# A Mamba-2 layer on one core: in the steps without an early convolution tile, the late tile is multiplied before the state's product

## The chip, the cores and the metric

One core of a Trainium2 chip. The time is the device time of one launch in microseconds (us), the median of three runs. TensorE is called PE in the profile (PEld is its weight load), VectorE is DVE, ScalarE is ACT, GpSimd is POOL and SyncE, which issues the transfers, is SP.

## The reference

The layer takes x of 2 batches by 1024 tokens by 512 channels, all float32, and returns x + s * g. Cut to what matters:

```python
xn = layernorm(x)
proj = xn @ in_proj_w.T                      # gate 4096, hbc 6144, dt 64
xBC = silu(conv_bias + sum_k pad(hbc)[k:k+L] * conv_weight[:, k])   # 4 taps over time
x, Bm, Cm = split(xBC)                       # 64 heads x 64, 8 groups x 128, 8 groups x 128
dt = softplus(dt + dt_bias); dA = exp(dt * -exp(A_log))
# over time, for each head:
state = state * dA_t + (dt_t * x_t) outer B_t
y_t = state @ C_t
y = y + x * D
yn = rms_norm_by_group(y) * norm_weight * silu(gate)
s = yn @ out_proj_w.T
g = silu(xn @ W.T + bias + lora(xn))
out = x + s * g
```

## The kernel before, in words

After a first stage (the first 125 us or so: layer norm, the gate g, the step sizes) the kernel runs a main loop of 128 steps i. A step is one chunk of 128 tokens of one group of 8 heads; 8 steps are the 1024 tokens of one group in one batch. In this document the groups are counted 0 to 15 in the order in which they run, and the place of a step in its group is 0 to 7: step i is group i // 8, place i % 8. Group 7 and group 8 differ from the others: in group 7 and the first steps of group 8 the finished rows of the first batch are also multiplied, added and stored by POOL (`fin_multiply`, `fin_add`), and the normalised input of the other batch is fetched.

Each engine runs its own instructions in the order in which they are written, and waits on semaphores for the others. The orders are written out by hand. In step i PE does, in this order:

- the output projection of chunk i-2 into `ps_out` (12 matmuls, waits for `ynt_hi` and `ynt_lo` of that chunk)
- `ps_y`, the outputs of chunk i-1 from the decay matrix and from the state before it (L1219, L1224; waits for `decay` by DVE L906 and for `cpre` by POOL L1027)
- the sum of squares of chunk i-2 (L1231), the transpose of B for chunk i (L1238)
- the early convolution tile, if the step has one (12 matmuls into `ps_conv`)
- a gate tile (12 matmuls into `ps_gate`)
- the state's product into `ps_s` (L1250, two matmul records of 128x512)
- the late convolution tile, if the step has one (12 matmuls into `ps_conv`)
- the transposes of x for chunk i+1 into `turned_x` (L1174), and C times B into `ps_g` (L1260)

Twelve matmuls are three passes of four (L1074, L1077, L1080 with L1081 for the last one), which is how a float32 product is made of split operands. The convolution's projection of the next block of 512 tokens has six tiles, spread over the four steps of the block before it: `conv_early(i)` gives one tile where i % 4 is 1, 2 or 3, `conv_late(i)` gives one where i % 4 is 0, 1 or 2. So steps at places 0 and 4 have a late tile and no early one, places 3 and 7 an early one and no late one, and places 1, 2, 5 and 6 have both. The last block of all has no next block, so steps 124 to 127 have no convolution tile.

The state's product of step i waits for `b_tok` (ACT), for `xw` (DVE L861) and for `S["state"]` of step i-1: the same bank `ps_s` holds the product of the step before until DVE has added it to the state (L872; L875 where the group begins). There is no `ps_s` product at place 7. DVE does in step i: the taps of the late tile of step i-1 (L753), `dtx` (L848), a scan of `decay` (L852), `last` (L857), `xw`, then for step i-1 `ps_y` plus `skip` (L866, waits for POOL's `skip`, L1056), `state` (L872), the product with the gate (L883), `out_sum` (L894), `ynt_lo` (L898), then the taps of the early tile and `decay` times `ps_g` (L906, waits for PE's L1260). POOL does in step i: `rstd_col` (L1009), the low halves of the weights where the place is 1, 3, 4, 5 or 6 (`wconv_lo` L918 of the next group at places 3 and 5, `wgate_lo` L924 at 4 and 6), `cpre`, two sums of squares (L1033, L1036), the decayed state (L1048) and `skip`. The convolution tile at place 4 is the first that needs the next group's `wconv_lo`.

Of the kernel before, what the change touches and what calls it, by code (L numbers as in the profile page):

```python
# [31 lines left out]
N = NB * CPB  # L32
# [55 lines left out]
def conv_early(i):  # L88

    nb, r = i // CPB + 1, i % CPB  # L90
    return nb * MT + 2 * r - 1 if r and nb < NB else None


def conv_late(i):
    nb, r = i // CPB + 1, i % CPB
    return nb * MT + 2 * r if r < CPB - 1 and nb < NB else None


def taps_done(k):

    return (TAPS - 1) * (k + 1)


def tile_of(k):
    nb, at = divmod(k, MT)
    m = tile_order(nb)[at]
    g, blk = nb // NBLK % GROUPS, nb % NBLK
    return nb, m, blk, g * MT + m
# [16 lines left out]
def build(nc, hidden, w_in_t, conv_w, conv_b, dt_bias, a_log, d_skip, norm_w, w_out_t,  # L125
          lora_a, lora_b_t, w_ffn_t, ffn_bias, lora_w, out):
    ctx = ExitStack()
    with ctx:
# [937 lines left out]
        def _(e):  # L1066
            w = Waits(e)

            def passes(ps, a, b, n, second, third, done):


                (a_hi, a_lo), (b_hi_, b_lo_) = a, b
                for t in range(n):
                    e.matmul(ps, a_hi(t), b_hi_(t), start=t == 0, stop=False)  # L1074
                second()
                for t in range(n):
                    e.matmul(ps, a_lo(t), b_hi_(t), start=False, stop=False)  # L1077
                third()
                for t in range(n - 1):
                    e.matmul(ps, a_hi(t), b_lo_(t), start=False, stop=False)  # L1080
                e.matmul(ps, a_hi(n - 1), b_lo_(n - 1), start=False, stop=True).then_inc(done, 1)  # L1081
# [17 lines left out]
            def conv(k):  # L1099
                nb, m, blk, tile = tile_of(k)  # L1100
                g = nb // NBLK
                ready = NCH + (blk + 1) * CPB
                if m < XT:
                    w.wait_ge(S["hi_cx"], KT * (g + 1))
                else:
                    w.wait_ge(S["hi_cbc"], KT * (g + 1))
                w.wait_ge(S["hi"], ready)
                if nb >= NB // 2:
                    w.wait_ge(landed_xn[blk], 32 * CPB)

                def w_lo_ready():
                    w.wait_ge(S["lo_cx"] if m < XT else S["lo_cbc"], KT * (g + 1))

                def xn_lo_ready():
                    w.wait_ge(S["lo"], ready)

                w.wait_ge(S["taps"], taps_done(k - 2))
                passes(ps_conv[k % 2][:, :], weights(wconv_hi, wconv_lo, chunk_cols(m)),
                       xn_cols(slice(blk * BLK, (blk + 1) * BLK)), KT, w_lo_ready, xn_lo_ready, S["mm_conv"])

            def rate(q, part):
                b, j = RATES[q]
                if part == 0:
                    ready = (0 if b == 1 else NCH) + (j + 1) * CPB
                    w.wait_ge(S["hi_dt"], KT)
                    w.wait_ge(S["hi"], ready)
                    w.wait_ge(S["z"], q)
                    passes(ps_out[:, :], weights(wout_hi, wout_lo, slice(0, P)),
                           xn_cols(slice(j * BLK, (j + 1) * BLK)), KT,
                           lambda: w.wait_ge(S["lo_dt"], KT), lambda: w.wait_ge(S["lo"], ready), S["mm_dt"])  # L1130
                elif part == 5:
                    ds = rate_rooms(q)[3]
                    w.wait_ge(S["pfx"], q + 1)
                    w.wait_ge(S["pt"], q)
                    if q == 3:
                        w.wait_ge(S["state"], 3)
                    for i in range(CPB - 1):
                        e.transpose(ps_s[:, i * P:(i + 1) * P], ds[:, i * P:(i + 1) * P], eye)
                    e.transpose(ps_s[:, (CPB - 1) * P:], ds[:, (CPB - 1) * P:], eye).then_inc(S["mm_pt"], 1)
# [52 lines left out]
            for i in range(N + DRAIN):  # L1192
                m, u = i - 1, i - DRAIN
                xb, cc = xc[i // CPB % 2], block_cols(i % NCH)
                cm, gm = m % NCH, group(m)
                if u >= 0:
                    gu = group(u)
                    w.wait_ge(S["z"], len(RATES))
                    w.wait_ge(S["osum"], u)
                    w.wait_ge(S["hi2"], u + 1)  # L1200
                    w.wait_ge(S["hi_out"], XT * (gu + 1))
                    passes(ps_out[:, :], (lambda t: ynt_hi[:, t, :], lambda t: ynt_lo[:, t, :]),
                           weights(wout_hi, wout_lo, slice(0, DM)), XT,
                           lambda: w.wait_ge(S["lo2"], u + 1), lambda: w.wait_ge(S["lo_out"], XT * (gu + 1)),
                           S["mm_out"])
                if 0 <= m < N:
                    mx, dx = decay[m % 3], dtx[m % 2]
                    w.wait_ge(S["M"], m + 1)
                    w.wait_ge(S["biased"], TOK)
                    w.wait_ge(S["dtx"], m + 1)  # L1210
                    w.wait_ge(S["lo2"], m)
                    if cm > 0:
                        w.wait_ge(S["state"], inner(m - 1))
                        w.wait_ge(S["cpre"], later(m))
                        before, c_left = state[(gm + cm - 1) % 2], cpre[(later(m) - 1) % 2]
                    for two in range(0, GH, 2):
                        for h in (two, two + 1):
                            y_h = ps_y[h % 2 * HD:(h % 2 + 1) * HD, h // 2 * P:(h // 2 + 1) * P]
                            mixed = e.matmul(y_h, dx[:, h * HD:(h + 1) * HD], mx[:, h * P:(h + 1) * P], start=True,  # L1219
                                             stop=cm == 0, skip_group_check=True)  # L1220
                        if cm > 0:
                            for h in (two, two + 1):
                                y_h = ps_y[h % 2 * HD:(h % 2 + 1) * HD, h // 2 * P:(h // 2 + 1) * P]
                                mixed = e.matmul(y_h, before[:, h * HD:(h + 1) * HD], c_left[:, h, :], start=False,  # L1224
                                                 stop=True, skip_group_check=True)
                    mixed.then_inc(S["mm_in"], 1)
                if u >= 0:
                    w.wait_ge(S["eye"], 3)
                    w.wait_ge(S["sum2"], u + 1)
                    w.wait_ge(S["M"], min(i, N))  # L1230
                    e.matmul(ps_g[:, 2 * P:2 * P + 1], square_sum[:, :], ones[:, :], start=True, stop=True,  # L1231
                             skip_group_check=True).then_inc(S["mm_ssq"], 1)
                if i < N and i % NCH < NCH - 1:
                    w.wait_ge(S["silu"], conv_no(i // CPB, XT) + 1)
                    w.wait_ge(S["M"], i)
                    w.wait_ge(S["var2"], u if u >= 0 else 0)
                    w.wait_ge(S["lo"], TOK)
                    e.transpose(ps_g[:, 0:P], xb[:, XT, cc], eye).then_inc(S["mm_bt"], 1)  # L1238
                if i < N and conv_early(i) is not None:
                    conv(conv_early(i))  # L1240
                for k in gated(i):
                    gate(k)
                if i == 3:
                    rate(3, 5)
                if i < N and i % NCH < NCH - 1:
                    w.wait_ge(S["pt"], 3 if i < 3 else 4)
                    w.wait_ge(S["b_tok"], inner(i))
                    w.wait_ge(S["xw"], inner(i))
                    w.wait_ge(S["state"], inner(m) if m >= 0 else 0)
                    e.matmul(ps_s[:, :], b_tok[:, :], xw[:, :], start=True, stop=True).then_inc(S["mm_u"], 1)  # L1250
                if i < N and conv_late(i) is not None:
                    conv(conv_late(i))
                if i + 1 < N:
                    turn_xc(i + 1)
                if i < N:
                    w.wait_ge(S["silu"], conv_no(i // CPB, XT + 1) + 1)
                    w.wait_ge(S["var2"], u + 1 if u >= 0 else 0)
                    if i % NCH < NCH - 1:
                        w.wait_ge(S["b_tok"], inner(i))
                    e.matmul(ps_g[:, P:2 * P], xb[:, XT, cc], xb[:, XT + 1, cc], start=True, stop=True,  # L1260
                             skip_group_check=True).then_inc(S["mm_g"], 1)
# [39 lines left out]
```

## Time and profile before

| | |
|---|---|
| median of 3 runs | 1868.99 us (1868.94 to 1869.1) |
| the profiled execution's own time | 1868.11 us |
| its span, first to last instruction | 1866.3 us |
| mean granted TensorE clock | 0.990 |
| PE busy | 96% of the span |
| PEld busy | 76% |
| DVE busy | 82% |
| POOL busy | 62% |
| ACT busy | 45% |
| PE's share of the chain that ended last | 77%, POOL 12% |

Busy time counts an instruction from its start to its end; the ends of matmuls are modelled and overlap the next one, so the distance from one start to the next is the better measure of what a matmul costs. "Idle before" in brackets is the time an engine stood still before an instruction, and the arrow names who released it.

### The profile page before, as it was taken

To read this page: it belongs to the slowest core of one execution; us is meant where nothing else is said; L and a number is where in the kernel's file an instruction comes from. 1 tells how busy PE (TensorE), PEld (TensorE's weight loads), DVE (VectorE), ACT (ScalarE), POOL (GpSimd) and SP (SyncE) were. 2 spreads that over 40 slices of the span, in tenths; PEclk is the share of its full clock that TensorE was granted. 3 is DMA by queue.
4 is the path that set the end of the run, shared out by engine and by line. 5 is a ranking of instruction groups with operands and counts; after the bars stand their busy time and mean duration, and the time that the engine had idled before them with its cause. 6 is when DMAs were issued, how large, how long until landed. Compare 5 with 4: busy or idle time off the path is not lost.

```text
span 1866.3 us, 29427 instructions
## 1 busy us (share of the span) xinstructions
PE 1799.7 (96%) x10904; PEld 1426.0 (76%) x10904; DVE 1524.5 (82%) x1960; ACT 835.2 (45%) x1806; POOL 1152.4 (62%) x1137
## 2 busy tenths in 40 slices
PE   6888999999999999999999999999999999999995
PEld 4766787878777777877777787777878788787874
DVE  6748788888888888888888878888888888888885
ACT  4865444443535444353534444354444435444431
POOL 4125757475575657566597756647574765857478
PEclk9998999999999999999999999999999999999998
DMA  7432423323232333323465333323233323323333
GB/s 246 151 103 70 148 77 130 102 102 106 98 136 102 102 102 102 124 95 132 148 203 181 119 113 108 119 91 115 89 116 111 124 103 102 135 77 106 102 114 124
DMA packets 113502, 220.70 MB, mean 118 GB/s; under 512 B 10448, under 2 KB 46672, under 8 KB 113360
## 3 DMA queue, kind: packets, MB, share of 16 engines
q1 hardware_dynamic: 112320, 218.66, 35.0%
q8 instruction: 87, 1.43, 0.3%
q14 instruction: 55, 0.45, 0.1%
q10 hardware_dynamic: 1040, 0.16, 0.0%
HBM read 204.63 MB, written 14.16 MB: 117 GB/s over the span
## 4 chain that ended last, share of the span: by engine, by line
PE 77%; POOL 12%; DVE 4%; issue 3%; ACT 2%; DMA 1%; SPq 0%; POOLq 0%; DVEq 0%; ACTq 0%
PE ps_conv L1074 9%; PE ps_conv L1077 8%; PE ps_conv L1080 6%; PE ps_y L1219 6%; PE ps_out L1074 5%; PE ps_out L1077 5%; PE ps_gate L1074 5%; PE ps_gate L1077 5%; PE ps_s L1250 4%; PE ps_y L1224 4%; PE ps_out L1080 4%; PE ps_gate L1080 4%; POOL wconv_lo L918 3%; PE turned_x L1174 2%; POOL state L1048 2%
## 5 line engine op out<-in xcount | busy, mean ns | idle before, releaser
L1009 POOL TENSOR_TENSOR rstd_col<-mean_square,half 128x1 f32<-128x1 f32 x128 | 107.2, 837 | 567.2 <-ACT mean_square L666 567.2
L753 DVE SCALAR_TENSOR_TENSOR xc<-ps_conv,convw_sb,xc 128x511 f32<-128x511 f32 (+2 forms) x576 | 429.6, 746 | 24.8 <-ACT xc L552 10.7
L906 DVE TENSOR_TENSOR decay<-decay,ps_g 128x1024 f32<-128x1024 f32 x128 | 156.0, 1218 | 199.0 <-PE ps_g L1260 199.0
L852 DVE TENSOR_TENSOR_SCAN decay<-decay,eye 128x1024 f32<-128x1024 f32 x128 | 297.8, 2327 | 0.8 <-DMA decay<-decays_d 0.8
L558 ACT ACTIVATE xc<-xc 128x512 f32<-128x512 f32 x192 | 121.3, 632 | 375.0 <-DVE xc L753 374.2
L1027 POOL TENSOR_TENSOR cpre<-cpre,xc 128x1024 f32<-128x1024 f32 x112 | 268.0, 2393 | 0.0
L1074 PE MATMUL ps_conv<-xn_hi,wconv_hi 128*128 128x512 f32 x768 | 256.3, 456 | 0.0
L1077 PE MATMUL ps_conv<-xn_hi,wconv_lo 128*128 128x512 f32 x768 | 207.2, 392 | 0.0
L1219 PE MATMUL ps_y<-decay,dtx 128*64 128x128 f32 x2048 | 197.3, 279 | 1.7 <-DVE decay L906 1.7
L1074 PEld LDWEIGHTS ps_conv<-xn_hi,wconv_hi 128*128 128x128 f32 x768 | 140.9, 193 | 62.9 <-issue 45.3
L675 ACT ACTIVATE square<-ps_y 128x512 f32<-128x512 f32 x128 | 76.7, 600 | 240.6 <-DVE ps_y L866 240.6
L1224 PE MATMUL ps_y<-cpre,state 128*64 128x128 f32 x1792 | 174.1, 273 | 0.0
L1077 PEld LDWEIGHTS ps_conv<-xn_hi,wconv_lo 128*128 128x128 f32 x768 | 144.9, 189 | 32.7
L1080 PE MATMUL ps_conv<-xn_lo,wconv_hi 128*128 128x512 f32 x576 | 162.3, 390 | 0.0
L1219 PEld LDWEIGHTS ps_y<-decay,dtx 128*64 128x64 f32 x2048 | 120.9, 136 | 48.4 <-issue 46.0
L1074 PE MATMUL ps_out<-wout_hi,ynt_hi 128*128 128x512 f32 x512 | 151.6, 418 | 4.6 <-DVE out_sum L894 4.6
L552 ACT ACTIVATE xc<-ps_conv,convb_sb,convw_sb 128x512 f32<-128x512 f32 (+1 forms) x192 | 150.2, 782 | 0.0
L1074 PE MATMUL ps_gate<-xn_hi,wgate_hi 128*128 128x512 f32 x512 | 141.4, 398 | 4.8 <-ACT wgate_hi L510 2.8
L918 POOL TENSOR_TENSOR wconv_lo<-stage,wconv_hi 128x512 fp32r<-128x512 f32 (+1 forms) x128 | 126.2, 1013 | 27.6 <-ACT wconv_hi L502 27.6
L1250 PE MATMUL ps_s<-xw,b_tok 128*128 128x512 f32 x224 | 118.9, 612 | 24.7 <-DVE state L872 16.8
L1077 PE MATMUL ps_out<-wout_hi,ynt_lo 128*128 128x512 f32 x512 | 140.8, 397 | 0.0
L1077 PE MATMUL ps_gate<-xn_hi,wgate_lo 128*128 128x512 f32 x512 | 138.0, 392 | 0.0
(192 smaller groups left out, 3743.8 us busy)
## 6 DMA issues: line engine op xcount, KB each, us to landing
decay<-decays_d SPq DMA_DIRECT2D x128, 512.0 KB, 5.2
cpre<-rows_d SPq DMA_DIRECT2D x112, 512.0 KB, 3.9
stage<-w_in_t SPq DMA_DIRECT2D x32, 1024.0 KB, 6.4
stage<-w_out_t SPq DMA_DIRECT2D x16, 1024.0 KB, 5.3
stage<-w_in_t SPq DMA_DIRECT2D x32, 256.0 KB, 3.4
out_sum<-hidden SPq DMA_DIRECT2D x16, 256.0 KB, 5.5
ffn_d<-sgate SPq DMA_DIRECT2D x16, 256.0 KB, 2.0
io<-ffn_d SPq DMA_DIRECT2D x16, 256.0 KB, 3.8
```

Of the source, the lines that this page charges most:

```text
L552: e.activation(acc[:, first:], ps[:, first:], ACT.Identity, bias=convb_sb[:, tile, 0:1], scale=tap).then_inc(S["tap0"], 1)
L753: e.scalar_tensor_tensor(acc[:, d:], ps[:, 0:BLK - d], convw_sb[:, tile, TAPS - 1 - d:TAPS - d], acc[:, d:], ALU.mult, ALU.add).then_inc(S ...
L852: e.tensor_tensor_scan(d[:, :], d[:, :], eye8[:, :, :].rearrange("p h i -> p (h i)"), 0.0, ALU.mult, ALU.add).then_inc(S["scan"], 1)
L906: e.tensor_tensor(by_head(d[:, :]), by_head(d[:, :]), ps_g[:, P:2 * P].unsqueeze(1).to_broadcast([P, GH, P]), ALU.mult).then_inc(S["M"], 1)
L918: e.tensor_tensor(lo[:, t, :], raw[:, t, :], hi[:, t, :].bitcast(F32), ALU.subtract).then_inc(done, 1)
L1027: e.tensor_tensor(cpre[k % 2][:, :, :], cpre[k % 2][:, :, :], xc[i // CPB % 2][:, XT + 1, block_cols(i % NCH)].unsqueeze(1).to_broadcast([ ...
L1074: e.matmul(ps, a_hi(t), b_hi_(t), start=t == 0, stop=False)
L1077: e.matmul(ps, a_lo(t), b_hi_(t), start=False, stop=False)
L1080: e.matmul(ps, a_hi(t), b_lo_(t), start=False, stop=False)
L1219: mixed = e.matmul(y_h, dx[:, h * HD:(h + 1) * HD], mx[:, h * P:(h + 1) * P], start=True, stop=cm == 0, skip_group_check=True)
L1224: mixed = e.matmul(y_h, before[:, h * HD:(h + 1) * HD], c_left[:, h, :], start=False, stop=True, skip_group_check=True)
L1250: e.matmul(ps_s[:, :], b_tok[:, :], xw[:, :], start=True, stop=True).then_inc(S["mm_u"], 1)
```

## The change

In a step that has a late convolution tile and no early one, the late tile's 12 matmuls are issued right after the gate tile, and the state's product behind them. In all other steps the order stays. Only PE's order changes; no instruction is added or removed, and each keeps its waits.

```diff
                 if i == 3:
                     rate(3, 5)
+                late_first = i < N and conv_early(i) is None and conv_late(i) is not None
+                if late_first:
+                    conv(conv_late(i))
                 if i < N and i % NCH < NCH - 1:
                     w.wait_ge(S["pt"], 3 if i < 3 else 4)
                     w.wait_ge(S["b_tok"], inner(i))
                     w.wait_ge(S["xw"], inner(i))
                     w.wait_ge(S["state"], inner(m) if m >= 0 else 0)
                     e.matmul(ps_s[:, :], b_tok[:, :], xw[:, :], start=True, stop=True).then_inc(S["mm_u"], 1)
-                if i < N and conv_late(i) is not None:
+                if i < N and conv_late(i) is not None and not late_first:
                     conv(conv_late(i))
```

## Rows read from the trace of the kernel before

**Rows 1.** The page's busy time of each engine, with its share of the span.

```profile
PE 1799.7 (96%) x10904; PEld 1426.0 (76%) x10904; DVE 1524.5 (82%) x1960; ACT 835.2 (45%) x1806; POOL 1152.4 (62%) x1137
```

**Rows 2.** Window over group 3: its length, then busy PE, PEld, DVE, ACT, POOL.

```profile
682.95:790.51 107.56, 106.97 (x662) 85.15 (x661) 90.06 (x114) 47.69 (x107) 67.37 (x68) 1.00 0.33 109
```

**Rows 3.** Who waited for whom, PE: total us, times, longest.

```profile
PE ps_s L1250 <- DVE state L872: 16.8, 18, 2.6
```

**Rows 4.** The chain that ended last, in order of time, group 2, places 3 and 4.

```profile
617.88 2.52 POOL wconv_lo L918 x2
...
626.94 1.04 POOL skip L1056
```

**Rows 5.** Timeline of PE at group 2, place 4: start, duration, instruction, idle before.

```profile
628.54 0.39 PE L1081 MATMUL ps_gate<-xn_lo,wgate_hi 128*128 128x512 f32 x1
629.52 1.10 PE L1250 MATMUL ps_s<-xw,b_tok 128*128 128x512 f32 x2 [0.59 <-DVE state L872]
630.05 1.49 PE L1074 MATMUL ps_conv<-xn_hi,wconv_hi 128*128 128x512 f32 x4
...
633.22 0.60 PE L1174 MATMUL turned_x<-eye,xc 128*128 128x128 f32 x4
```

**Rows 6.** Timeline of PE at place 4 of group 0 and of group 8, same two ends.

```profile
197.82 0.39 PE L1081 MATMUL ps_gate<-xn_lo,wgate_hi 128*128 128x512 f32 x1
...
202.86 0.60 PE L1174 MATMUL turned_x<-eye,xc 128*128 128x128 f32 x4
...
1059.39 0.39 PE L1081 MATMUL ps_gate<-xn_lo,wgate_hi 128*128 128x512 f32 x1
...
1064.53 0.60 PE L1174 MATMUL turned_x<-eye,xc 128*128 128x128 f32 x4
```

**Rows 7.** Timeline of PE at group 3, place 0, same two ends.

```profile
682.71 0.40 PE L1081 MATMUL ps_gate<-xn_lo,wgate_hi 128*128 128x512 f32 x1
...
686.55 0.60 PE L1174 MATMUL turned_x<-eye,xc 128*128 128x128 f32 x4
```

**Rows 8.** Timeline of PE at group 2, place 7: a gate tile behind a convolution tile.

```profile
671.62 1.07 PE L1074 MATMUL ps_gate<-xn_hi,wgate_hi 128*128 128x512 f32 x4
...
674.34 0.60 PE L1174 MATMUL turned_x<-eye,xc 128*128 128x128 f32 x4
```

**Rows 9.** Timeline of PE at group 2, place 3: the transposes behind the state's product.

```profile
619.29 1.02 PE L1250 MATMUL ps_s<-xw,b_tok 128*128 128x512 f32 x2
...
620.15 0.60 PE L1174 MATMUL turned_x<-eye,xc 128*128 128x128 f32 x4
```

**Rows 10.** Timeline of DVE and POOL from group 2, place 4 on.

```profile
628.69 0.68 DVE L872 TENSOR_TENSOR state<-ps_s,state 128x512 f32<-128x512 f32 x1
...
630.81 0.69 DVE L898 TENSOR_TENSOR ynt_lo<-ps_y,ynt_hi 128x512 fp32r<-128x512 f32 x1
...
634.08 1.22 DVE L906 TENSOR_TENSOR decay<-decay,ps_g 128x1024 f32<-128x1024 f32 x1 [2.58 <-PE ps_g L1260]
...
635.51 1.04 POOL L1056 TENSOR_TENSOR skip<-xc,dskip_sb 128x512 f32<-128x512 f32 x1
...
638.03 2.28 DVE L852 TENSOR_TENSOR_SCAN decay<-decay,eye 128x1024 f32<-128x1024 f32 x1
...
640.55 0.69 DVE L861 TENSOR_TENSOR xw<-turned_x,last 128x512 f32<-128x512 f32 x1
```

**Rows 11.** Timeline of POOL, PE and DVE in group 7, places 4 and 6.

```profile
956.30 2.42 POOL L1027 TENSOR_TENSOR cpre<-cpre,xc 128x1024 f32<-128x1024 f32 x1
...
959.52 0.44 PE L1219 MATMUL ps_y<-decay,dtx 128*64 128x128 f32 x4
...
986.72 1.22 DVE L906 TENSOR_TENSOR decay<-decay,ps_g 128x1024 f32<-128x1024 f32 x1 [0.46 <-PE ps_g L1260]
```

**Rows 12.** Timeline at group 2, place 3: POOL's decayed state and DVE's scan.

```profile
623.70 2.44 DVE L852 TENSOR_TENSOR_SCAN decay<-decay,eye 128x1024 f32<-128x1024 f32 x1
...
623.96 3.02 POOL L1048 TENSOR_TENSOR state<-state,total_bc 128x512 f32<-128x512 f32 x1
```

## Prediction

> **What bounds the kernel now.** I read the page first: PE is busy 96% of the span, DVE 82%, POOL 62% [rows 1]. That makes PE the first candidate, but a share over the whole span hides where it stands still, so I went to windows of one group each. An ordinary group takes 107.56 us with PE busy for 106.97: 0.59 us of idle time in eight steps [rows 2]. So in the main loop the time is PE's instruction stream plus very few gaps, and the question is which gaps the change touches.
>
> The list of waits names the largest kind: the state's product waited for DVE's `state` (L872) 18 times, 16.8 us in all [rows 3]. I went through its timeline: 15 of the 18 stand at place 4, one in each of groups 0 to 14 (0.98 in group 0, 0.58 or 0.59 in thirteen groups, 1.05 in group 8). The three others are at step 2 (2.64) and at places 5 and 6 of the last group (2.49 and 2.00), and those steps keep their order. Place 4 stalls because it has only the gate tile ahead of the product, and because POOL is late there. The chain that ended last goes through POOL's `wconv_lo` until 620.40, then its other work up to `skip` until 627.98 [rows 4], DVE's `ps_y` and `state`, which ends at 628.69 + 0.68 = 629.37 [rows 10], and the product at 629.52 [rows 5].
>
> **The change, part by part.** Nothing is added or removed, so the sum consists of starts that move. I measure from the start of the gate tile's last matmul to the start of the transposes that close the sequence.
>
> Before, at an ordinary place 4: 628.54 to 633.22 = 4.68 us [rows 5]. The same instructions at place 0, where nothing waits: 682.71 to 686.55 = 3.84 [rows 7]. So the wait costs 4.68 - 3.84 = 0.84 in starts, more than its 0.59 of idle time, because idle time is counted only from the modelled end of the matmul before.
>
> After: a convolution tile straight behind a gate tile is in no row of this kernel. The nearest is the opposite, a gate tile behind a convolution tile at place 7, with the same shapes: 12 matmuls from 671.62 to 674.34, 2.72, or 0.227 each [rows 8]. From the gate tile's last start to the product are thus 13 such distances, 2.95. From the product to the transposes behind it, place 3 shows 619.29 to 620.15 = 0.86 [rows 9]. Together 3.81, if nothing waits. At place 0 that is 0.03 less than 3.84. The bound from below for the new handovers is no saving against 3.84. The other bound is that a convolution tile keeps the length that it has now behind the product: 630.05 to 633.22 is 3.17 [rows 5] instead of 2.72, so up to 0.45 a step more. I take 3.81, since rows 8 show two tiles of the same kind one behind the other.
>
> Now the wait. The product would start at 628.54 + 2.95 = 631.49, and `state` ends at 629.37: 2.1 us to spare, so all of the wait goes. Per place:
>
> - 13 ordinary groups: 4.68 - 3.81 = 0.87, times 13 = 11.3
> - group 0: 197.82 to 202.86 is 5.04 [rows 6]; minus 3.81 = 1.2
> - group 8: 1059.39 to 1064.53 is 5.14 [rows 6]; minus 3.81 = 1.3
> - place 0 in 16 groups: 16 x 0.03 = 0.5
> - sum: 14.3 us
>
> **What comes next where the stall was.** PE runs 0.87 ahead from place 4 on, and something could stop it there. The second pass of the output projection needs `ynt_lo`, finished at 630.81 + 0.69 = 631.50 [rows 10]; by then PE is only at the product. DVE's L906 stood idle 2.58 us waiting for PE [rows 10], so DVE moves ahead by the whole 0.87. POOL's `skip` for the next `ps_y` ends at 636.55 and DVE asks for it after `xw`, 641.24 before and 640.37 after [rows 10]. What waits for the product itself is DVE's `xw` of the next step (it may not be overwritten) and then `state`: the product ends at about 632.3, `xw` starts at 640.55 - 0.87 [rows 10], 7.3 us later. The tile that is moved ahead needs `wconv_lo`, ready at 620.40 [rows 4], against 628.77. No transfer is issued by PE and none waits for the product, so SP's queue keeps its order.
>
> Group 7 is tighter, because POOL also finishes the output rows there. At place 4 `cpre` ends at 958.72 and `ps_y` starts at 959.52; 0.87 earlier is 958.65 [rows 11], a new wait of 0.1. At place 6 DVE's L906 idles only 0.46 [rows 11], so DVE can follow PE by 0.46 and not by 0.87, and 0.4 is at stake at the next `ps_y`. I take 0.1 for group 7, and 0.5 as the other end.
>
> The row of the decayed state at place 3 shows POOL held up by DVE: it takes 3.02 us and overlaps the scan of 2.44 [rows 12], where `skip`, of the same size, takes 1.04 [rows 10]. Now DVE moves 0.87 against POOL, whose work around place 4 stays. The scan moves from 638.03 to 637.16 and `skip` ends at 636.55, so they stay apart by 0.6. The Trainium skill, page "SBUF — State Buffer", section "Who interferes with whom", says that a DVE instruction with two SBUF inputs and a GpSimd one that reads SBUF take turns, the later one blocked for the whole of the first. The trace agrees (3.02 against 1.04). By that rule the new overlap would be in group 7, where the sum would lose up to about another 0.5; it speaks against this change there and nowhere else.
>
> **The sum.** 14.3 - 0.1 = 14.2 us. The profiled execution took 1868.11 and would take 1853.9; the median of the runs shown is 0.88 above it, 1868.99, and I give the prediction against that: 1854.8 us, 0.76% less. From no change a measurement of this kernel can tell about 0.2%, 3.7 us.
>
> **The rivals.**
>
> - Only the idle time comes back: at place 4 PE regains the 0.98 + 13 x 0.59 + 1.05 = 9.7 us that the profile calls idle, because the 0.25 a step between idle time and starts is spent at the new handovers. For it: handovers at the product do cost something in each order (a tile of 3.17 behind it, or 0.86 to the transposes). Against it: rows 7 and 9 add up without it. 1859.3 us.
> - The convolution tile keeps its 3.17 wherever it stands: 31 steps have it (places 0 and 4, without the last), 31 x 0.45 = 14.0, which eats nearly all of the 14.2. 1868.8 us, the same as before. The slow start is seen only right behind the product, so I hold this for unlikely. A stall absorbed by the next wait would give the same time; I found no such wait.
> - On the other side: the product is now 2.7 us later in all 31 steps, and DVE's `xw` and `state` wait for it in each. It decides where the 7.3 us to spare are gone. Were DVE 8 us nearer, the wait would be 0.7 in 31 steps, 21.7 us, minus 14.2: 1876.5 us. Against it: `xw` waits today for the scan, which waits for `ps_g` and the taps, and those come after the product in either order.
>
> **How the numbers follow.** The forecast gets 0.80, the idle time alone 0.09, the same as before 0.07, the later product 0.04. The range begins at 1852.5: the forecast with a further 2.3 us, about what the wait at step 2 (2.64) could give if DVE's work in group 0 moved ahead too. It ends at 1859.5, the first rival, which takes in the 1 us that group 7 could lose. It leaves out 0.11 of the rivals and a little of the forecast. Faster by over 0.2% has 0.89 (the forecast and the first rival), within 0.2% 0.07, slower 0.04.
>
> **What the profile afterwards would show.** The waits of L1250 for L872 fall from 18 to 3, 16.8 to 7.1 us. An ordinary group takes 106.7 instead of 107.56 us. From the gate's last matmul to the transposes are 3.8 us at places 0 and 4, and the convolution tile there takes 2.7. L906 at place 4 idles about 1.7 instead of 2.58. I am wrong if `ps_y` at place 5, or the output projection, shows a wait that was not there, or if group 7 keeps its length.

## Result, and the profile after

The changed kernel takes 1854.58 us (median of 6 runs, 1854.35 to 1857.16) against 1868.97 of the kernel before (median of 6). The ratio is 0.9928, with a 95% interval of 0.9917 to 0.9940. The prediction was 1854.8 us, in a range of 1852.5 to 1859.5.

One correction to the names first. By the count of this document the rows that stand above under group 2 belong to group 4, and those under group 3 to group 5: the product that waits at place 4 starts at 199.19, 306.75, 414.34, 521.92 and 629.52 us in groups 0 to 4. All of these but group 0 are ordinary groups, so the distances hold. The names below are the right ones.

The profiled execution took 1854.72 us. First the page's busy time, to be held against [rows 1]: the same work in 13.4 us less.

```profile
span 1852.9 us, 29427 instructions
PE 1795.4 (97%) x10904; PEld 1427.2 (77%) x10904; DVE 1524.6 (82%) x1960; ACT 831.2 (45%) x1806; POOL 1156.4 (62%) x1137
```

Then who waited for whom on PE, against [rows 3]. The product's line is now L1253. Of the 18 waits for `state` 3 are left, those at step 2 and at the end of the last group.

```profile
PE ps_s L1253 <- DVE state L872: 7.1, 3, 2.6
PE ps_s L1253 <- DVE state L875: 6.3, 1, 6.3
```

Windows one group long, over an ordinary group (group 5) and over group 8 (each begins 0.5 to 0.9 us ahead of the transposes that close place 0; length, then busy PE, PEld, DVE, ACT, POOL; the first answers to [rows 2]). In the ordinary group PE no longer stands still at all.

```profile
681.40:788.08 106.68, 106.68 (x662) 85.22 (x661) 90.08 (x113) 47.39 (x108) 67.39 (x68) 1.00 0.33 109
1001.33:1108.83 107.50, 106.90 (x663) 85.13 (x661) 91.77 (x113) 47.91 (x109) 75.64 (x74) 1.00 0.35 122
```

Now PE's timeline at group 4, place 4, which answers to [rows 5].

```profile
624.78 0.39 PE L1081 MATMUL ps_gate<-xn_lo,wgate_hi 128*128 128x512 f32 x1
625.01 1.07 PE L1074 MATMUL ps_conv<-xn_hi,wconv_hi 128*128 128x512 f32 x4
627.50 0.40 PE L1081 MATMUL ps_conv<-xn_lo,wconv_hi 128*128 128x512 f32 x1
627.74 1.03 PE L1253 MATMUL ps_s<-xw,b_tok 128*128 128x512 f32 x2
628.60 0.60 PE L1174 MATMUL turned_x<-eye,xc 128*128 128x128 f32 x4
```

From the gate's last matmul to the transposes are 3.82 us, where there were 4.68. The tile takes 627.74 - 625.01 = 2.73, so it has lost its slow start, and the product has 0.86 to itself. DVE's timeline around it, against [rows 10]:

```profile
624.34 0.70 DVE L866 TENSOR_TENSOR ps_y<-ps_y,skip 128x512 f32<-128x512 f32 x1 [0.35 <-POOL skip L1056]
624.95 0.68 DVE L872 TENSOR_TENSOR state<-ps_s,state 128x512 f32<-128x512 f32 x1
...
629.46 1.22 DVE L906 TENSOR_TENSOR decay<-decay,ps_g 128x1024 f32<-128x1024 f32 x1 [1.69 <-PE ps_g L1263]
```

DVE still waits for POOL's `skip`, as before, and `state` still ends just behind the gate tile (625.63). What has changed is that PE does something else meanwhile: the product starts 2.11 us after `state` has ended. The stall has not moved; its cause is still there and is covered.

**Where the time came from.** I took the start of the transposes that close place 0 of each group in both traces and compared the distances. Up to those of step 0: 135.01 before, 135.23 after, 0.2 lost (in the first stage, which the change does not touch). Group 0: 121.18 and 119.93, 1.25 gained. Groups 1 to 14: 1507.16 and 1494.65, 12.51 gained. The rest: 102.95 and 103.11, 0.16 lost. Together 13.4, the difference of the spans. Thirteen of the places 4 gained 0.83 to 0.86 each, group 0's gained 1.23 and group 8's 1.15; places 0 gained 0.02 to 0.03 each (0.05 in group 0), places 3 gained 0.02 and places 1 and 5 0.01. Group 7 gave back 0.22 at place 5, and group 8 gave back 0.15 at place 2.

### The profile page after: what moved, and what is told of

Its sections match the earlier page's. It is cut to its first block, busy times and chain, and to the rows that moved or that the text cites. A ratio compares the mean times of both kernels' runs of the same rounds, so it can differ in the third digit from the quotient of the medians.

```text
span 1852.9 us, 29427 instructions
## 1 busy us (share of the span) xinstructions
PE 1795.4 (97%) x10904; PEld 1427.2 (77%) x10904; DVE 1524.6 (82%) x1960; ACT 831.2 (45%) x1806; POOL 1156.4 (62%) x1137
## 4 chain that ended last, share of the span: by engine, by line
PE 85%; DVE 5%; POOL 4%; ACT 3%; issue 2%; DMA 1%; SPq 0%; POOLq 0%; DVEq 0%; ACTq 0%
PE ps_conv L1074 9%; PE ps_conv L1077 9%; PE ps_conv L1080 6%; PE ps_y L1219 6%; PE ps_gate L1074 6%; PE ps_gate L1077 6%; PE ps_out L1074 6%; PE ps_out L1077 6%; PE ps_y L1224 5%; PE ps_s L1253 5%; PE ps_gate L1080 4%; PE ps_out L1080 4%; PE turned_x L1174 3%; PE ps_conv L1081 2%; PE ps_g L1231 2%
## 5 line engine op out<-in xcount | busy, mean ns | idle before, releaser
L906 DVE TENSOR_TENSOR decay<-decay,ps_g 128x1024 f32<-128x1024 f32 x128 | 155.9, 1218 | 183.3 <-PE ps_g L1263 183.3
L1074 PE MATMUL ps_conv<-xn_hi,wconv_hi 128*128 128x512 f32 x768 | 243.2, 439 | 0.0
L1056 POOL TENSOR_TENSOR skip<-xc,dskip_sb 128x512 f32<-128x512 f32 x128 | 133.6, 1043 | 0.0
```

Of the source, the lines that this page charges most:

```text
L906: e.tensor_tensor(by_head(d[:, :]), by_head(d[:, :]), ps_g[:, P:2 * P].unsqueeze(1).to_broadcast([P, GH, P]), ALU.mult).then_inc(S["M"], 1)
L1056: e.tensor_tensor(turns(skip), xc[nb % 2][:, 0:XT, block_cols(i % NCH)], dskip_sb[:, gi * XT:(gi + 1) * XT].unsqueeze(2).to_broadcast([P, ...
```

## The experiments

All were timed beside the kernel before on the same chip: its median was 1868.91, 1868.30 and 1868.39 us in the three sets (runs 1 to 4, 5 to 8, 9 to 11). "Ordinary group" is the distance between the transposes that close place 0 of one ordinary group and of the next. It was 107.58 us before and 106.69 in the changed kernel, and it is the finest measure here, since it repeats within 0.04 us from group to group (107.57 to 107.60 before, within 0.01 after).

### 1 and 2: place 4 alone, place 0 alone

```diff
-late_first = i < N and conv_early(i) is None and conv_late(i) is not None
+late_first = i < N and conv_early(i) is None and conv_late(i) is not None and i % NCH == 4   # run 2: == 0
```

> The late tile goes first only at place 4 of a group (15 steps), place 0 keeps the old order. Theory (the gain is the wait for the state, which stands only at place 4): 13.1 of the 13.6 us of the full change stay, time 1855.2 us; from the gate's last matmul to the transposes 3.8 us at place 4, 3.84 at place 0. Rival (the gain comes from cheaper handovers between the tiles, in all 31 steps alike): 15 of 31 steps, about half, 1862 us.

> The late tile goes first only at place 0 of a group (16 steps). Theory: only the handover changes, 0.03 us a step, 0.5 in all, 1868.5 us, not to be told from before; the 15 waits of about 0.6 us at place 4 stay. Rival (handovers): half of the gain, 1862 us.

Place 4 alone: 1855.29 us, ratio 0.9928 [0.9915, 0.9941], ordinary group 106.73. Place 0 alone: 1868.40 us, ratio 0.9998 [0.9989, 1.0007], ordinary group 107.54. The parts add up: 0.85 and 0.04 of the 0.89. So the fifteen steps with a wait carry the gain, and the handovers are worth what the starts of [rows 7 to 9] said. That "only the idle time comes back" falls as well: 0.85 is the loss in starts, not the 0.59 called idle.

### 3 and 4: POOL's skip made later, before and after the change

```diff
+                    if i % NCH == 3:
+                        e.tensor_tensor(turns(skip), ...same operands..., ALU.mult).then_inc(S["extra"], 1)
+                        w.wait_ge(S["extra"], i // NCH + 1)
                     e.tensor_tensor(turns(skip), ...).then_inc(S["skip"], 1)
```

> The kernel before, with POOL's skip computed twice at place 3 (the same values, about 1.04 us more, plus about 0.1 for its own semaphore). Theory: the wait at place 4 is set by POOL's skip, so it grows by 1.1 us in 15 groups: 1869.0 + 16.5 = 1885.5 us. Rival (the profile names the wrong releaser, and POOL has slack there): 1869 us.

> The changed kernel with the same extra POOL work at place 3. Theory: the product now has 2.1 us to spare and the output projection about as much, so 1.1 us of delay is hidden in the ordinary groups; groups 7 and 8, where POOL is tighter, may pay up to 1 us each: 1854.6 to 1857 us. Rival (the change only moved the wait to the next user of POOL's result, and there is no room left): 15 x 1.1 us more, 1871 us.

With the order of before: 1885.71 us, ratio 1.0091 [1.0075, 1.0107]. Its timeline at group 2, place 4, first POOL, then PE:

```profile
413.13 1.04 POOL L1057 TENSOR_TENSOR skip<-xc,dskip_sb 128x512 f32<-128x512 f32 x1
414.25 1.04 POOL L1061 TENSOR_TENSOR skip<-xc,dskip_sb 128x512 f32<-128x512 f32 x1
...
416.83 1.10 PE L1255 MATMUL ps_s<-xw,b_tok 128*128 128x512 f32 x2 [1.71 <-DVE state L872]
```

I had expected 1885.5. The wait was 0.59 there and is 1.71: the 1.12 us that POOL takes longer arrive whole at PE, and an ordinary group takes 108.71, 1.13 more. That is the chain from POOL over DVE to PE, shown by lengthening it. With the order of after, the ordinary group takes 106.68, the same as without the extra work: the 2.1 us to spare cover all of it. The whole kernel took 1858.78, ratio 0.9945 [0.9932, 0.9958], 1.8 above the upper end of what I expected. Two places make most of it in the profiled execution. Group 7 took 109.10 instead of 106.91, and group 0 122.23 instead of 119.93. I had allowed 1 us for group 7; it lost 2.2, in one step:

```profile
955.14 0.44 PE L1224 MATMUL ps_y<-decay,dtx 128*64 128x128 f32 x4 [1.02 <-POOL cpre L1027]
955.46 2.36 DVE L852 TENSOR_TENSOR_SCAN decay<-decay,eye 128x1024 f32<-128x1024 f32 x1
955.76 2.32 POOL L1036 TENSOR_TENSOR square_sum<-square 128x128 f32<-128x128 f32 x1
958.13 0.38 PE L1236 MATMUL ps_g<-ones,square_sum 128*128 128x1 f32 x2 [1.02 <-POOL square_sum L1036]
```

First PE waits for `cpre`, as in the changed kernel but longer. Then POOL's `square_sum`, which takes 0.46 elsewhere, starts 0.3 us behind DVE's scan, takes 2.32, and PE waits for it. The Trainium skill, page "SBUF — State Buffer", section "Who interferes with whom", says that of a DVE instruction with two SBUF inputs and a GpSimd one that reads SBUF the later one is blocked for the whole of the first. The rows agree: the scan ends at 957.82, and `square_sum` 0.26 later.

### 5 and 6: POOL's skip made earlier, before and after the change

```diff
+                (skip of step i, as below)
                 if 0 <= m < N and cm < NCH - 2:
                     (decayed state of step i-1)
-                if i < N:
-                    (skip of step i)
```

> The kernel before, with POOL's skip ahead of the decayed state instead of behind it. Theory: skip is ready about 1 us earlier, DVE's ps_y at place 4 then starts when xw is done instead of 0.35 us later, so the wait at place 4 shrinks by 0.35 us in 15 groups and no more: 1869.0 - 5.2 = 1863.8 us. What is left of the wait, about 0.24, is DVE's own chain. Rival (POOL's order is the whole of it): the wait is gone and the time is that of the changed kernel, 1855 us.

> The changed kernel with POOL's skip ahead of the decayed state. Theory: nothing waits for skip at place 4 any more, so it brings nothing in ordinary groups; in groups 7 and 8 up to 0.5 each: 1853.6 to 1854.6 us. Rival (the two edits add): 5 us less, 1849.4 us.

Before, with `skip` first: 1862.59 us, ratio 0.9970 [0.9959, 0.9981], ordinary group 107.14, so 0.44 less instead of the 0.35 that I expected. First DVE and POOL at group 4, where POOL is at the `skip` of place 3 and DVE at the scan of place 4, then PE at place 4:

```profile
622.36 2.45 DVE L852 TENSOR_TENSOR_SCAN decay<-decay,eye 128x1024 f32<-128x1024 f32 x1
622.62 3.02 POOL L1043 TENSOR_TENSOR skip<-xc,dskip_sb 128x512 f32<-128x512 f32 x1
624.84 0.82 DVE L857 TENSOR_TENSOR last<-decay,prefix_dt 128x8 f32<-128x8 f32 x1
...
627.20 0.39 PE L1082 MATMUL ps_gate<-xn_lo,wgate_hi 128*128 128x512 f32 x1
627.74 1.10 PE L1251 MATMUL ps_s<-xw,b_tok 128*128 128x512 f32 x2
...
631.43 0.60 PE L1175 MATMUL turned_x<-eye,xc 128*128 128x128 f32 x4
```

The list of waits does not name a wait here any more, yet 627.20 to 631.43 is 4.23, still 0.39 above the 3.84 of [rows 7]: the product starts 0.54 behind the gate's last matmul instead of 0.24, inside the modelled end of that matmul. So half of the loss was DVE's wait for `skip`, and the other half stands in DVE's chain from the scan to `state`; this order of POOL's does not remove it. That second half need not be DVE's own work. Run 5 only puts `skip` where the decayed state was, beside the scan, and both engines are still held up there: `skip` takes 3.02 us instead of 1.04, DVE's scan 2.45 instead of 2.28, and `last`, which runs until `skip` is done, 0.82 instead of 0.17. In the kernel before, `last` took 0.82 to 0.83 at place 4 of every ordinary group too, and 0.17 at the places around it. By these rows DVE loses 0.82 us (0.17 and 0.65), more than the 0.39 that is left. An order that keeps POOL's work of place 3 clear of the scan might have removed the whole wait; no run tried it. Together with the change, `skip` first brings nothing in the ordinary group (106.68), so the two edits do not add; they cure the same wait. Its time was 1856.99 us, ratio 0.9935 [0.9923, 0.9948], above the 1853.6 to 1854.6 that I expected: its profiled execution has 122.20 in group 0, of which more below.

### 7 and 8: the late tile first everywhere, and the product still later

```diff
-late_first = i < N and conv_early(i) is None and conv_late(i) is not None
+late_first = i < N and conv_late(i) is not None          # run 7
```

In run 8 the 31 changed steps issue gate, late tile, transposes, C times B, and the product last.

> The late tile goes ahead of the product in every step that has one, also where there is an early tile (places 1, 2, 5, 6). Theory: in groups 1 to 14 there is no wait to cover there, so only the handover is saved, 0.02 to 0.03 us in 61 steps, 1.5 us; at steps 1 and 2 the waits of 6.3 and 2.6 us for the state are covered by up to 2.9 us each, of which DVE, which is the bound there, gives back part: 3 us. Together 1850 us. Rival (the product in all steps later than DVE can bear): slower than 1855 us.

> The changed kernel, but in the 31 changed steps the product stands behind the transposes and the C times B product too, last in the step. Theory: xw of the next step had 7.3 us to spare and now has 6.5, nothing waits, and the C times B product is 0.9 us earlier for DVE, which is not the bound: 1854.6 us plus or minus 1 for other handovers. Rival (a later product is what costs): slower by some 0.5 us a step, 1870 us.

Run 7: 1852.47 us, ratio 0.9916 [0.9903, 0.9930], 2.1 below the changed kernel, where I had expected 1850 and so 4.6. An ordinary group takes 106.59, 0.09 less, which is all handover: its window shows PE busy throughout, as it was already. Its waits for `state`:

```profile
PE ps_s L1253 <- DVE state L872: 6.5, 3, 2.5
PE ps_s L1253 <- DVE state L875: 2.9, 1, 2.9
```

The wait at step 1 falls from 6.3 to 2.9, but group 0 as a whole takes 119.34 against 119.93: PE is 4 to 5 us ahead at steps 1 and 2 and waits for DVE afterwards, 2.5 us for `out_sum` (L891) in a wait that the changed kernel does not have, and 3.1 us for L906 where there were 1.9.

Run 8: 1857.34 us, ratio 0.9935 [0.9921, 0.9948]. The ordinary group takes 106.70, so a product that is later by another 0.9 us costs nothing there, and the rival in which the later product costs is off the table. The whole kernel misses what I expected, 1853.6 to 1855.6, by 1.7 us; its profiled execution has the excess in group 0 (122.11, see the last section) and in group 7. Windows over groups 7 and 8 of run 8:

```profile
897.16:1005.18 108.02, 106.85 (x663) 85.25 (x661) 91.51 (x113) 47.38 (x108) 85.60 (x79) 1.00 0.61 196
1005.18:1111.86 106.68, 106.68 (x663) 85.22 (x662) 91.78 (x113) 47.40 (x108) 73.94 (x71) 1.00 0.37 122
```

Group 8 loses its last waits (107.50 in the changed kernel), with C times B coming earlier for DVE: the 0.60 us for L906 at `ps_y` is not in its list of waits. Group 7 loses 1.1 by the same collision as in run 4, this time with no extra work in the kernel:

```profile
955.50 2.38 DVE L852 TENSOR_TENSOR_SCAN decay<-decay,eye 128x1024 f32<-128x1024 f32 x1
955.80 2.32 POOL L1036 TENSOR_TENSOR square_sum<-square 128x128 f32<-128x128 f32 x1
...
958.18 0.38 PE L1231 MATMUL ps_g<-ones,square_sum 128*128 128x1 f32 x2 [1.02 <-POOL square_sum L1036]
```

### 9 to 11: both ends, and all together

Run 9 is the changed kernel with the product last in steps 124 to 126. Run 10 is the changed kernel with the late tile first at steps 1 and 2 too. Run 11 has the late tile first everywhere and the product last in steps 124 to 126.

```diff
+product_last = i < N and conv_early(i) is None and conv_late(i) is None     # runs 9 and 11
+late_first = i < N and conv_late(i) is not None and (conv_early(i) is None or i in (1, 2))     # run 10
```

> The changed kernel, and in steps 124 to 126 (the last group's steps without any convolution tile) the product stands last in the step, behind the transposes and the C times B product. Theory: two waits for the state are left there, 2.49 and 2.00 us, and the 1.0 us of PE work that is put ahead of each covers that much if DVE is not itself the bound there: at best 2 us less, 1852.6; since DVE and not PE paces those steps, more likely 1 us, 1853.6. Rival (DVE paces the end alone): no difference.

> The changed kernel, and at steps 1 and 2 too the late tile goes ahead of the product. Theory: PE covers 2.7 us of the 6.3 us wait at step 1 (the run with the late tile first everywhere showed 2.9 left), but DVE paces these steps and the gain is back to within 1 us by step 4: 1853.5 to 1854.6. Rival (it adds up): 1852 us or less.

> The late tile first in every step that has one, and the product last in steps 124 to 126. Theory: the handover is about 0.025 us cheaper in each of the 61 further steps, 0.09 us in an ordinary group as the run before showed, 1.4 in all, and what the end gives: 1851 to 1853 us, the fastest of all. Rival: no difference from the changed kernel, 1854.6.

Run 9: 1856.42 us, ratio 0.9935 [0.9922, 0.9949], not the 1852.6 to 1853.6 of my theory. Of the waits for `state` 3.2 us are left instead of 7.1, but PE now waits for `xw` instead. From the transposes of place 0 of the last group to the end of the span it is 103.02 against 103.11 us: DVE paces the end alone, and the rival in my expectation was right. The whole is 1.8 above the changed kernel, with 122.23 in group 0 of the profiled execution. Run 10: 1853.97, ratio 0.9921 [0.9908, 0.9935], group 0 119.44, as expected: what PE gains at step 1 it waits for afterwards. Run 11: 1852.70, ratio 0.9914 [0.9900, 0.9927], the same as run 7 within the scatter. Runs 7 and 11 are the fastest kernels here; against the changed kernel they bring some 2 us, 0.1%, which is less than its own executions differ by (2.8), and the intervals of the ratios overlap. What is clear of the scatter is the ordinary group, 106.59 in both against 106.69.

## Why the prediction was right

- **The wait.** Fifteen waits at place 4 were to go, with 16.8 us falling to 7.1. They did, to the tenth of a us. Runs 1 and 3 show the cause: the fifteen steps alone bring 0.85 of the 0.89 us of an ordinary group, and lengthening POOL's work lengthens the wait by the same 1.12.
- **The length of the new sequence.** Worked out as 13 distances of 0.227 and 0.86, 3.81 us; it is 3.82. The order was in no row before, but each neighbour pair had a near relative in [rows 8 and 9]. Runs 1 and 2 separate it: 0.85 from the wait, 0.04 from the handover.
- **The margins.** `state` has 2.11 us to spare (2.1 forecast), L906 idles 1.69 (1.7 forecast), `ps_y` waits for `cpre` 0.15 in group 7 (0.1 forecast). This last one is a new wait of `ps_y` at place 5, which I had named as a sign of being wrong; it stands in group 7 alone, where I had priced it. The rival of the later product says that it comes 2.7 us later in all 31 steps; that holds at place 0 (2.96 instead of 0.23 behind the gate's last matmul), while at an ordinary place 4 it is 2.0 (2.96 instead of 0.98). Run 4 shows that the 2.1 are real: 1.1 us more of POOL's work vanish in them.
- **The sum.** 14.2 us forecast, 13.4 in the profiled executions and 14.4 between the medians. The largest term that was off is group 8: 1.15 instead of 1.3 at place 4, since PE there waits for L906 at `ps_y` just before, 0.60 us where it was 0.43, and another 0.15 is lost at place 2. Group 7 gave back 0.22 instead of 0.1. The rest is 0.2 lost ahead of step 0 and 0.16 behind place 0 of the last group, neither of which was in the sum. That the median came out within 0.2 us of the forecast is in part luck: the sum was 0.8 too high for the profiled executions, and six executions of the changed kernel spread over 2.8 us.
- **POOL and DVE in each other's way.** I had priced a new overlap at up to 0.5 in group 7; no row gives that figure. The overlap was not new there. In the kernel before it held up `skip`, behind place 4 of group 7, and in the changed kernel it holds up the decayed state instead, the instruction in front of it (first before, then after):

```profile
960.79 2.32 DVE L852 TENSOR_TENSOR_SCAN decay<-decay,eye 128x1024 f32<-128x1024 f32 x1
960.92 3.02 POOL L1056 TENSOR_TENSOR skip<-xc,dskip_sb 128x512 f32<-128x512 f32 x1
...
953.47 3.13 POOL L1048 TENSOR_TENSOR state<-state,total_bc 128x512 f32<-128x512 f32 x1
953.48 2.28 DVE L852 TENSOR_TENSOR_SCAN decay<-decay,eye 128x1024 f32<-128x1024 f32 x1
```

Which of the two started first, starts 0.01 us apart do not tell. DVE then waits 0.35 us for `skip`, which it did not before, and PE hardly notices. Runs 4 and 8 show that the risk was larger than my price: when the overlap hits `square_sum`, for which PE waits directly, it costs 1 us at once.

## What to carry to other kernels

Where an in-order engine waits a little for another one at the same place in each round, look for independent work that stands right behind the wait, and issue it first; it costs nothing if the delayed instruction's own users have room, which is read from their starts. Measure such a wait from start to start against an undisturbed instance of the same sequence, not by the idle time: it was 0.84 and not 0.59 here, and in run 5 0.39 of loss had no entry among the waits. To learn whether a wait is gone or only covered, lengthen its cause: run 3 passed on all of it, run 4 none in the ordinary groups. And when a wait is explained by an engine's own chain, compare the duration of each of its instructions with the same instruction elsewhere: `last` with 0.82 instead of 0.17 was the sign that the chain was itself held up.

## What I had not expected of the hardware

The six executions of the changed kernel lie between 1854.35 and 1857.16 us, and the five of run 6 at 1854.4 and 1854.9 or at 1857.0 to 1857.4. Only one execution of each kernel was profiled, so the place of such a difference is seen only between kernels, and there it is group 0: in the profiled executions it took 119.3 to 119.9 us (the changed kernel, runs 1, 7, 10 and 11) or 122.1 to 122.2 (runs 4, 6, 8 and 9), with ordinary groups behind that are alike to 0.15 us. It goes with where the granted TensorE clock drops to half, after PE had stood still for several us at steps 1 and 2. Windows of 10 us (length, PE busy, granted clock, DMA share, GB/s) of the changed kernel, then of run 9:

```profile
165.00:175.00 10.00, 7.37 (x24) 0.83 0.29 62
...
185.00:195.00 10.00, 8.40 (x64) 1.00 0.28 89
```

```profile
165.00:175.00 10.00, 7.35 (x31) 1.00 0.16 38
...
185.00:195.00 10.00, 7.94 (x31) 0.83 0.17 39
```

A window at 0.83 has a third of its length at 1.2 GHz instead of 2.4. In the changed kernel that falls beside step 2, where PE waits for DVE anyway; in run 9 it falls some 20 us later. The late drop stands in all four kernels with 122.1 to 122.2 and in none of the five others. But it does not explain the whole: a third of 10 us at half clock can cost PE at most 1.7 us, not 2.3. And run 3 has the late drop too, and its group 0 took 122.45, only 1.27 more than the 121.18 of the kernel before, of which 1.1 is POOL's extra work. That the drop is what costs is my reading of the rows, and it stays open. The executions of run 6 alone show both levels of time, so the order of instructions can hardly decide it by itself, if the drop is what parts them; no run sets the place of the drop. Comparisons of a few us between kernels are therefore better read from the ordinary groups than from the medians.
